# A graph network's last stage: all row gathers before all row scatters on one queue, and an earlier sum over the heads

## The chip, the cores and the metric

One core of one Trainium2 chip runs the kernel. Times are device microseconds of that core; the profile is of one execution, with times in microseconds from the start of its span. Engines: PE (matmuls and transposes), the vector engine (DVE), ACT (activations), POOL (here it only issues indirect DMAs), and SP (issues plain DMAs).

## The reference, cut to what matters

Two graph layers over 50,000 nodes of 96 features and 25,000 edges whose `dst` is sorted.

1. A message layer: rows of `x` at `src` and 32 edge features give messages and gates, their products are summed by `dst`, a small network updates each node, and two layer norms follow (the layer's own, then that of `x +` its output). The result is `x1`.
2. An attention layer, then a last norm:

```python
K, Q, V = x1 @ Wk + bk, x1 @ Wq + bq, x1 @ Wv + bv        # 8 heads of 12
E = edge_attr_96 @ We + be
score = exp(clip(sum_over_head(K[src] * Q[dst] / sqrt(12) * E), -5, 5))
h = segment_sum(V[src] * score, dst) / (segment_sum(score, dst) + 1e-6)
out = layernorm(x1 + h)
```

A node without an edge has h = 0; its output needs no attention and is written by the node update itself.

## The kernel before, in words

Edges go in 49 groups of 512, each as 4 tiles of 128 rows; nodes go in 49 groups of 1024. One SBUF array, `rows`, has a place for every tile of edges (196 tiles of 128 x 96).

The work has three compute stages (`edge_step`, `update_step`, `attend_step`, in each engine's block), and POOL's program is five passes over the 49 groups, four indirect DMAs of 128 rows for each group, written out without loops:

- line 375: rows of x at src into `rows` (edge stage);
- line 384: sums out of `rows` into `agg_d` at the last edge of each dst;
- line 398: rows of x1 at dst into `rows`. The two counts that say how many node groups must have been stored before it are read from SBUF into registers at the top of each group (`need_x1`);
- lines 410 and 420: the last stage, quoted below. It gathers rows of x1 at src for group g into `x1s` (four places in `x_in`, so it waits until PE has transposed group g - 4), and, eight groups behind, scatters the finished rows `fin` (four more places in `x_in`) of group g - 8 to `out`. Before the first scatter it waits until the node update has stored all of its own output.

```python
LAG = 8
for g in range(EGROUPS + LAG):
    if g < EGROUPS:
        if g >= XSLOTS:
            pool.wait_ge(ops_turned, 3 * (g - XSLOTS + 1))
        ...
    b = g - LAG
    ...
    if b >= 0:
        pool.wait_ge(fin_made, b + 1)
```

The attention stage itself takes one group a step. SP loads `x1d` (a copy of the group's part of `rows`, line 339), `ea` (edge features, line 344) and a mask (line 349, after the scan two groups back). PE, in `attend_step(i)`: K, Q, E and V products of group i (lines 557 to 566; V waits for the scan of group i - 1), the transposes back of the group before (line 572), twelve transposes of group i + 1 (helper `turn`, line 431: four of x1s, four of x1d, four of ea), and then the sum over the heads of `kqe` (line 586). ACT adds the bias to K (689), makes the final rows of group i - 3 (696), copies the three sets of transposes from PSUM (706), and takes exp (711). The vector engine makes `kq` (959), `kqe` (973), the division by the sums (988), the clip of the summed heads (998), the residual (1004), the norm's statistics (1009), the weighing of V (1016) and the running segment sum, a scan (1026), which carries over from group to group. Small operations of the norm are laid between them.

The update stage uses six double arrays of 128 x 768, `hg`, `xb`, `y`, `agg_in`, `x1o` and `oo`; nothing reads or writes them in the attention stage.

Of the kernel before, what the change touches and what calls it, by code (L numbers as in the profile page):

```python
# [25 lines left out]
P = 128  # L26
# [4 lines left out]
EJ = 4  # L31
# [13 lines left out]
XSLOTS = 4  # L45
FAR = 1 << 20
# [26 lines left out]
def per_slot(i, slot):  # L73

    return i * 8 + (16 - 8 * slot)
# [7 lines left out]
def build(nc, x, src, dst, ea32, ea96, mW1, mb1, mW2, mb2, gW1, gb1, gW2, gb2, uW1, ub1, uW2, ub2,  # L83
          ln_g, ln_b, Wq, bq, Wk, bk, We, be, Wv, bv, ident_c, heads_c, spare_c, bounds_c, out):
    with ExitStack() as ctx:
        def sb(name, shape, dt=F32):
            return ctx.enter_context(nc.sbuf_tensor(name, shape, dt))
# [37 lines left out]
        agg_in = sb("agg_in", [P, 2, NJ * D])  # L125
# [6 lines left out]
        hg, xb, y = (sb(n, [P, 2, NJ * D]) for n in ("hg", "xb", "y"))  # L132
        x1o, oo = sb("x1o", [P, 2, NJ * D]), sb("oo", [P, 2, NJ * D])
# [17 lines left out]
        x1s, fin = (x_in[:, :, k * EJ * D:(k + 1) * EJ * D].rearrange("p s (j f) -> p s j f", j=EJ) for k in range(2))  # L151
# [74 lines left out]
        lnb_placed = sem("lnb_placed")  # L226
        out_scattered = [[sem(f"out_scattered{t}_{j}") for j in range(EJ)] for t in range(2)]
# [21 lines left out]
        def _(sp):  # L249
# [83 lines left out]
            def attend_step(i, s, inner):  # L333
                if inner or i + 1 < EGROUPS:
                    if inner or i >= 1:
                        sp.wait_ge(ops_turned, i * 3)
                    for j in range(EJ):
                        sp.wait_ge(xd_gathered[1 - s][j], per_slot(i + 1, 1 - s))
                    sp.dma_start(x1d[:, 1 - s, :, :], rows[:, bass.DynSlice(i * EJ + EJ, EJ), :]).then_inc(x1d_loaded[1 - s], 16)
                    if isinstance(i, int) and i + 1 == EFULL:  # L340
                        sp.dma_start(ea[:, 1 - s, 0:ETAIL_J, :], ea96[EFULL * EROWS:TFULL * P, :].rearrange("(j p) f -> p j f", p=P)).then_inc(ea_loaded[1 - s], 16)
                        sp.dma_start(ea[0:ETAIL_P, 1 - s, ETAIL_J, :], ea96[TFULL * P:E, :]).then_inc(ea_loaded[1 - s], 16)
                    else:
                        sp.dma_start(ea[:, 1 - s, :, :], ea96[bass.DynSlice(i * EROWS + EROWS, EROWS), :].rearrange("(j p) f -> p j f", p=P)).then_inc(ea_loaded[1 - s], 16)
                if inner or i + 1 < EGROUPS:
                    sp.wait_ge(cont_stored, 48)
                    if inner or i >= 1:
                        sp.wait_ge(cscanned, i)
                    sp.dma_start(mask[:, 1 - s, :], cont_d[:, bass.DynSlice(i * EROWS + EROWS, EROWS)].broadcast_to([DH, EROWS])).then_inc(cmask_loaded[1 - s], 16)

            sweep(sp, -1, EGROUPS - 1, 3, 1, attend_step)
# [7 lines left out]
        def _(pool):  # L359
# [26 lines left out]

            pool.wait_ge(needs_made, 1)
            for g in range(EGROUPS):

                needs = [pool.value_load(need_x1[0:1, s, g:g + 1], min_val=16, max_val=slot_total(0)) for s in range(2)]  # L390
                for j in range(EJ):
                    pool.wait_ge(agg_added[g % 2][j], per_slot(g, g % 2))
                    if g >= 2:
                        pool.wait_ge(xd_gathered[g % 2][j], per_slot(g - 2, g % 2))
                for s in range(2):
                    pool.wait_ge(x1_stored[s], needs[s])
                for j in range(EJ):
                    pool.indirect_dma_start(rows[:, g * EJ + j, :], None, x1_d, rows_at(dst_at, g, j)).then_inc(xd_gathered[g % 2][j], 16)  # L398
            for s in range(2):
                pool.wait_ge(x1_stored[s], slot_total(s))  # L400

            LAG = 8
            for g in range(EGROUPS + LAG):
                if g < EGROUPS:
                    if g >= XSLOTS:
                        pool.wait_ge(ops_turned, 3 * (g - XSLOTS + 1))
                    for j in range(EJ):
                        if g >= 2:
                            pool.wait_ge(x1s_gathered[g % 2][j], per_slot(g - 2, g % 2))
                        pool.indirect_dma_start(x1s[:, g % XSLOTS, j, :], None, x1_d, rows_at(src_i, g, j)).then_inc(x1s_gathered[g % 2][j], 16)  # L410
                b = g - LAG
                if b == 0:
                    for s in range(2):
                        pool.wait_ge(out_stored[s], slot_total(s))
                if b >= 0:
                    pool.wait_ge(fin_made, b + 1)
                    for j in range(EJ):
                        if b >= 2:
                            pool.wait_ge(out_scattered[b % 2][j], per_slot(b - 2, b % 2))
                        pool.indirect_dma_start(out, rows_at(put_at, b, j), fin[:, b % XSLOTS, j, :], None,  # L420
                                                bounds_check=N - 1, oob_is_err=False).then_inc(out_scattered[b % 2][j], 16)
# [7 lines left out]
        def _(pe):  # L429
# [119 lines left out]

            def attend_step(i, q, inner):  # L550
# [23 lines left out]
                if inner or i + 1 < EGROUPS:  # L574
                    for j in range(EJ):
                        pe.wait_ge(x1s_gathered[1 - s][j], per_slot(i + 1, 1 - s))
# [15 lines left out]
        def _(act):  # L592
# [90 lines left out]
            def attend_step(i, q, inner):  # L683
# [6 lines left out]
                if inner or i >= 3:  # L690
                    act.wait_ge(cnorm_ready, i - 2)
                    if inner or i >= 7:
                        for j in range(EJ):
# [374 lines left out]
```

## Time and profile before

| what | value |
|---|---|
| runs of the kernel | 1256.85 us median of 3 (1254.91 to 1256.98) |
| the profiled execution | 1256.61 us, span 1254.8 us |
| busy: PE / DVE / ACT / POOL | 1030.6 / 956.2 / 688.5 / 946.5 us |
| granted PE clock, mean | 0.911 of full speed |
| packets of POOL's queue / SP's queue | 31,360 with 44.13 MB / 131,213 with 149.31 MB |
| POOL's last stage | from 750.49 us to the end |

The page gives busy time, not limits: an engine that is busy 80% may wait for another, and one that is busy 75% may have no pause that anything could fill. A group line tells the busy time and mean duration of like instructions, then the idle time of their engine just before them with what ended it; "issue" is idle time for which the profile shows no wait. A timeline line has start, duration, engine, line, operation, what is written and read, how many were merged, and in brackets the idle time before it.

### The profile page before, as it was taken

To read this page: it belongs to the slowest core of one execution; us is meant where nothing else is said; L and a number is where in the kernel's file an instruction comes from. 1 tells how busy PE (TensorE), PEld (TensorE's weight loads), DVE (VectorE), ACT (ScalarE), POOL (GpSimd) and SP (SyncE) were. 2 spreads that over 40 slices of the span, in tenths; PEclk is the share of its full clock that TensorE was granted. 3 is DMA by queue.
4 is the path that set the end of the run, shared out by engine and by line. 5 is a ranking of instruction groups with operands and counts; after the bars stand their busy time and mean duration, and the time that the engine had idled before them with its cause. 6 is when DMAs were issued, how large, how long until landed. Compare 5 with 4: busy or idle time off the path is not lost. (4 is left out here: it accounts for less than half of the span.)

```text
span 1254.8 us, 25004 instructions
## 1 busy us (share of the span) xinstructions
PE 1030.6 (82%) x5213; PEld 670.0 (53%) x5213; DVE 956.2 (76%) x4292; ACT 688.5 (55%) x1522; POOL 946.5 (75%) x984
## 2 busy tenths in 40 slices
PE   5999999989999999999999307788778877887770
PEld 2555555548877777777777303444444444443330
DVE  3544444437999999999999944888888788888883
ACT  2554545522687877778787743444444444444441
POOL 6777777777777777777777777777777777777777
PEclk9999999989999999999999758888888888888885
DMA  6787887544566666766677453334334333333320
GB/s 173 229 230 223 229 233 216 127 133 119 155 219 199 214 214 198 226 213 225 210 226 226 141 167 88 95 95 110 93 92 107 98 93 97 103 96 93 96 74 29
DMA packets 165371, 194.57 MB, mean 155 GB/s; under 512 B 102463, under 2 KB 111024, under 8 KB 165314
## 3 DMA queue, kind: packets, MB, share of 16 engines
q1 hardware_dynamic: 131213, 149.31, 38.4%
q0 software_dynamic: 31360, 44.13, 14.4%
q10 hardware_dynamic: 2740, 0.60, 0.3%
q14 instruction: 50, 0.40, 0.1%
q8 instruction: 8, 0.13, 0.0%
HBM read 101.21 MB, written 77.56 MB: 142 GB/s over the span
## 5 line engine op out<-in xcount | busy, mean ns | idle before, releaser
L384 POOL DMA_INDIRECT agg_d<-rows,put_at x196 | 193.5, 987 | 59.8 <-issue 47.3
L420 POOL DMA_INDIRECT out<-x_in,put_at x196 | 192.9, 984 | 59.7 <-issue 55.1
L410 POOL DMA_INDIRECT x_in<-agg_d,src_i x196 | 188.2, 960 | 62.0 <-issue 56.4
L398 POOL DMA_INDIRECT rows<-agg_d,dst_at x196 | 186.1, 950 | 62.4 <-issue 54.5
L375 POOL DMA_INDIRECT rows<-in_x,src_i x196 | 185.6, 947 | 62.4 <-issue 59.1
L658 ACT ACTIVATE x1o<-y,nshift,nscale 128x96 f32<-128x96 f32 x392 | 145.6, 454 | 87.5 <-DVE nshift L913 87.3
L696 ACT ACTIVATE x_in<-yc,cshift,cscale 128x96 f32<-128x96 f32 x196 | 75.5, 456 | 163.3 <-DVE cshift L1033 123.2
L431 PE MATMUL ps<-ident,x_in 128*96 128x128 f32 x588 | 93.8, 302 | 55.3 <-DMA x_in<-agg_d,src_i 54.1
L790 DVE SCALAR_TENSOR_TENSOR ps<-hidden,ps 96x512 f32<-96x512 f32 x49 | 33.9, 691 | 124.8 <-ACT hidden L637 124.8
L566 PE MATMUL ps<-nT,Wvs 96*104 96x512 f32 x98 | 59.3, 689 | 78.3 <-DVE seg L1026 78.2
L522 PE MATMUL ps<-uW2s,nT 97*128 97x96 f32 x784 | 98.6, 279 | 21.0 <-ACT nT L678 21.0
L870 DVE BATCH_NORM_STATS2 bn<-ps 128x6 f32<-128x96 f32 x392 | 100.3, 261 | 16.4 <-PE ps L522 16.1
L664 ACT ACTIVATE oo<-x1o,nscale 128x96 f32<-128x96 f32 x392 | 112.7, 361 | 0.0
L522 PEld LDWEIGHTS ps<-uW2s,nT 97*128 97x128 f32 x784 | 91.2, 191 | 31.8 <-ACT nT L678 31.8
L533 PEld LDWEIGHTS ps<-ident,agg_in 128*96 128x96 f32 x784 | 91.3, 163 | 26.7 <-issue 26.7
L431 PEld LDWEIGHTS ps<-ident,x_in 128*96 128x96 f32 x588 | 74.2, 142 | 56.8 <-issue 56.2
L888 DVE SCALAR_TENSOR_TENSOR y<-hg,nscale,xb 128x96 f32<-128x96 f32 x392 | 102.2, 311 | 0.6 <-issue 0.3
L530 PE MATMUL ps<-einT,uW1x 96*96 96x512 f32 x196 | 97.2, 619 | 1.2 <-ACT einT L650 1.2
L539 PE MATMUL ps<-centre,einT 96*128 96x96 f32 x784 | 94.2, 273 | 0.0
L533 PE MATMUL ps<-ident,agg_in 128*96 128x128 f32 x784 | 93.9, 273 | 0.0
L924 DVE BATCH_NORM_STATS2 bn<-y 128x6 f32<-128x96 f32 x392 | 93.7, 252 | 0.2 <-issue 0.2
L539 PEld LDWEIGHTS ps<-centre,einT 96*128 96x128 f32 x784 | 91.4, 192 | 0.0
(147 smaller groups left out, 2248.1 us busy)
## 6 DMA issues: line engine op xcount, KB each, us to landing
agg_d<-zeros SPq DMA_DIRECT2D x40, 480.0 KB
x_in<-in_x SPq DMA_DIRECT2D x49, 384.0 KB
agg_in<-agg_d SPq DMA_DIRECT2D x49, 384.0 KB
agg_d<-x1o SPq DMA_DIRECT2D x49, 384.0 KB
out<-oo SPq DMA_DIRECT2D x49, 384.0 KB
mask<-cont_d SPq DMA_DIRECT2D x49, 208.0 KB
ein<-rows SPq DMA_DIRECT2D x49, 192.0 KB
mask<-cont_d SPq DMA_DIRECT2D x49, 192.0 KB
```

Source lines behind the costliest of these rows:

```text
L375: pool.indirect_dma_start(rows[:, g * EJ + j, :], None, x, rows_at(src_i, g, j)).then_inc(xs_gathered[g % 2][j], 16)
L384: pool.indirect_dma_start(agg_d, rows_at(put_at, g, j), rows[:, g * EJ + j, :], None, bounds_check=N - 1, oob_is_err=False).then_inc(agg_a ...
L398: pool.indirect_dma_start(rows[:, g * EJ + j, :], None, x1_d, rows_at(dst_at, g, j)).then_inc(xd_gathered[g % 2][j], 16)
L410: pool.indirect_dma_start(x1s[:, g % XSLOTS, j, :], None, x1_d, rows_at(src_i, g, j)).then_inc(x1s_gathered[g % 2][j], 16)
L420: pool.indirect_dma_start(out, rows_at(put_at, b, j), fin[:, b % XSLOTS, j, :], None, bounds_check=N - 1, oob_is_err=False).then_inc(out_s ...
L431: mmx = pe.transpose(to, of, ident[:, :])
L522: m = pe.matmul(ps[:, 4 + 2 * s + j // 4, (j % 4) * D:(j % 4 + 1) * D], nT[:, s, j * P:(j + 1) * P], uW2s[:, :], start=False, stop=j % 4 == 3)
L533: m = pe.matmul(ps[0:D, 2 + j // 4, (j % 4) * P:(j % 4 + 1) * P], agg_in[:, 1 - s, j * D:(j + 1) * D], ident[:, :], start=False, stop=j % ...
L539: m = pe.matmul(ps[:, 4 + 2 * (1 - s) + j // 4, (j % 4) * D:(j % 4 + 1) * D], xT[:, j // 4, (j % 4) * P:(j % 4 + 1) * P], centre[:, :], st ...
L658: o = act.activation(x1o[:, s, j * D:(j + 1) * D], y[:, s, j * D:(j + 1) * D], ACT.Identity, bias=nshift[:, k, j:j + 1], scale=nscale[:, k ...
L664: o = act.activation(oo[:, 1 - s, j * D:(j + 1) * D], x1o[:, 1 - s, j * D:(j + 1) * D], ACT.Identity, scale=nscale[:, k, 2, j:j + 1])
L888: b = dve.scalar_tensor_tensor(y[:, s, at], hg[:, s, at], nscale[:, 1 - s, 0, j:j + 1], xb[:, s, at], ALU.mult, ALU.add)
```

## The change

POOL's last stage becomes two passes. The gathers of x1 at src run for all groups first, into 24 places named `ahead` that lie over the six update arrays (now one array `node_work`, in the order hg, xb, y, agg_in, x1o, oo); the first 16 places need hg, xb, y and agg_in to be free, and the wait for the update's own output moves to group 16. From group 24 on a gather waits until group g - 24 has been copied away. SP copies each group from its place in `ahead` to the four places of `x1s` by a plain DMA (new semaphores `x1s_loaded`), between its copies for x1d and ea, and PE waits for that copy instead of the gather. All scatters follow in a second pass. ACT writes its final rows into `rows`, in the place of their group, and the scatters read them there; ACT's wait for earlier scatters is gone.

On PE, the sum over the heads of group i comes after the first four of the twelve transposes of group i + 1, not after all twelve. In the pass at dst, POOL reads the next group's two counts behind the first two gathers of a group. SP's attention loop is written out.

```diff
-        agg_in = sb("agg_in", [P, 2, NJ * D])
...
-        hg, xb, y = (sb(n, [P, 2, NJ * D]) for n in ("hg", "xb", "y"))
-        x1o, oo = sb("x1o", [P, 2, NJ * D]), sb("oo", [P, 2, NJ * D])
+        node_work = sb("node_work", [P, 6, 2, NJ * D])
+        hg, xb, y, agg_in, x1o, oo = (node_work[:, k, :, :] for k in range(6))
...
-            def attend_step(i, s, inner):
...
+            for g in range(EGROUPS):
+                s = g % 2
+                if g >= 2:
+                    sp.wait_ge(ops_turned, (g - 1) * 3)
+                for j in range(EJ):
+                    sp.wait_ge(xd_gathered[s][j], per_slot(g, s))
+                sp.dma_start(x1d[:, s, :, :], rows[:, g * EJ:(g + 1) * EJ, :]).then_inc(x1d_loaded[s], 16)
+                for j in range(EJ):
+                    sp.wait_ge(x1s_gathered[s][j], per_slot(g, s))
+                sp.dma_start(x1s[:, g % XSLOTS, :, :], ahead[:, g % AHEAD, :, :]).then_inc(x1s_loaded[g % XSLOTS], 16)
...
             pool.wait_ge(needs_made, 1)
+            needs = [need_of(0, s) for s in range(2)]
             for g in range(EGROUPS):
-
-                needs = [pool.value_load(need_x1[0:1, s, g:g + 1], min_val=16, max_val=slot_total(0)) for s in range(2)]
...
                 for j in range(EJ):
                     pool.indirect_dma_start(rows[:, g * EJ + j, :], None, x1_d, rows_at(dst_at, g, j)).then_inc(xd_gathered[g % 2][j], 16)
+                    if j < 2 and g + 1 < EGROUPS:
+                        needs.append(need_of(g + 1, j))
...
-            LAG = 8
-            for g in range(EGROUPS + LAG):
...
+            for g in range(EGROUPS):
+                if g == AHEAD_FREE:
                     for s in range(2):
                         pool.wait_ge(out_stored[s], slot_total(s))
-                if b >= 0:
...
+                if g >= AHEAD:
+                    pool.wait_ge(x1s_loaded[(g - AHEAD) % XSLOTS], per_slot4(g - AHEAD, (g - AHEAD) % XSLOTS))
+                for j in range(EJ):
+                    if g >= 2:
+                        pool.wait_ge(x1s_gathered[g % 2][j], per_slot(g - 2, g % 2))
+                    pool.indirect_dma_start(ahead[:, g % AHEAD, j, :], None, x1_d, rows_at(src_i, g, j)).then_inc(x1s_gathered[g % 2][j], 16)
+
+            for g in range(EGROUPS):
+                pool.wait_ge(fin_made, g + 1)
+                for j in range(EJ):
+                    if g >= 2:
+                        pool.wait_ge(out_scattered[g % 2][j], per_slot(g - 2, g % 2))
+                    pool.indirect_dma_start(out, rows_at(put_at, g, j), rows[:, g * EJ + j, :], None,
+                                            bounds_check=N - 1, oob_is_err=False).then_inc(out_scattered[g % 2][j], 16)
...
                     for b, (of, t) in enumerate(((x1s, (q + 1) % XSLOTS), (x1d, 1 - s), (ea, 1 - s))):
+                        if b == 1:
+                            sum_heads(i, inner)
                         for j in range(EJ):
                             turn(ps[0:D, b, j * P:(j + 1) * P], of[:, t, j, :], ops_turned if j == EJ - 1 else None)
-                if inner or 0 <= i < EGROUPS:
-                    pe.wait_ge(kqe_made, i + 1)
-                    pe.matmul(ps[0:DH, 5, :], heads[:, :], kqe[:, :], start=True, stop=True).then_inc(heads_summed, 1)
+                else:
+                    sum_heads(i, inner)
...
-                    if inner or i >= 7:
-                        for j in range(EJ):
-                            act.wait_ge(out_scattered[1 - s][j], per_slot(i - 7, 1 - s))
                     for j in range(EJ):
-                        o = act.activation(fin[:, (q + 1) % XSLOTS, j, :], yc[:, 1 - s, j, :], ACT.Identity,
+                        o = act.activation(rows[:, bass.DynSlice(i * EJ - 3 * EJ + j, 1), :].rearrange("p a f -> p (a f)"), yc[:, 1 - s, j, :], ACT.Identity,
```

## Rows read from the trace of the kernel before

**Rows 1.** Page, first lines: span, busy time of each engine and its share.
```profile
span 1254.8 us, 25004 instructions
...
PE 1030.6 (82%) x5213; PEld 670.0 (53%) x5213; DVE 956.2 (76%) x4292; ACT 688.5 (55%) x1522; POOL 946.5 (75%) x984
```

**Rows 2.** Page, groups by line, POOL's passes; busy, mean ns, idle before.
```profile
L384 POOL DMA_INDIRECT agg_d<-rows,put_at x196 | 193.5, 987 | 59.8 <-issue 47.3
L420 POOL DMA_INDIRECT out<-x_in,put_at x196 | 192.9, 984 | 59.7 <-issue 55.1
L410 POOL DMA_INDIRECT x_in<-agg_d,src_i x196 | 188.2, 960 | 62.0 <-issue 56.4
L398 POOL DMA_INDIRECT rows<-agg_d,dst_at x196 | 186.1, 950 | 62.4 <-issue 54.5
```

**Rows 3.** Timeline of POOL, start of the last stage: start us, us, what, idle before.
```profile
750.49 0.94 POOL L410 DMA_INDIRECT x_in<-agg_d,src_i  x1 [0.30 <-issue]
...
789.26 0.94 POOL L410 DMA_INDIRECT x_in<-agg_d,src_i  x1 [0.30 <-issue]
792.75 0.94 POOL L410 DMA_INDIRECT x_in<-agg_d,src_i  x1 [2.54 <-PE ps L431]
```

**Rows 4.** Timeline of POOL, gathers and scatters in turn.
```profile
1156.12 1.01 POOL L420 DMA_INDIRECT out<-x_in,put_at  x1 [0.30 <-issue]
1157.43 0.99 POOL L420 DMA_INDIRECT out<-x_in,put_at  x1 [0.30 <-issue]
1158.73 0.97 POOL L420 DMA_INDIRECT out<-x_in,put_at  x1 [0.30 <-issue]
...
1161.28 0.99 POOL L410 DMA_INDIRECT x_in<-agg_d,src_i  x1 [0.30 <-issue]
...
1166.35 1.01 POOL L420 DMA_INDIRECT out<-x_in,put_at  x1 [0.30 <-issue]
```

**Rows 5.** Timeline of POOL, the last scatters.
```profile
1211.18 0.97 POOL L420 DMA_INDIRECT out<-x_in,put_at  x1 [0.30 <-DMA out<-x_in,put_at]
...
1252.06 0.97 POOL L420 DMA_INDIRECT out<-x_in,put_at  x1 [0.30 <-issue]
```

**Rows 6.** Timeline of the vector engine, four of the 49 scans.
```profile
771.13 1.22 DVE L1026 TENSOR_TENSOR_SCAN seg<-mask,ps 104x512 f32<-104x512 f32 x1
...
796.41 1.28 DVE L1026 TENSOR_TENSOR_SCAN seg<-mask,seg,ps 104x512 f32<-104x512 f32 x1
...
806.08 1.28 DVE L1026 TENSOR_TENSOR_SCAN seg<-mask,seg,ps 104x512 f32<-104x512 f32 x1
...
1226.39 1.28 DVE L1026 TENSOR_TENSOR_SCAN seg<-mask,seg,ps 104x512 f32<-104x512 f32 x1
```

**Rows 7.** Timeline of PE: x1d transposes and heads of a step.
```profile
799.92 1.06 PE L431 MATMUL ps<-ident,x1d 128*96 128x128 f32 x4
...
801.63 1.43 PE L586 MATMUL ps<-hidden,heads 96*104 96x512 f32 x2
```

**Rows 8.** Timeline of the vector engine, same step: kqe, clip, weighing.
```profile
798.77 0.74 DVE L973 SCALAR_TENSOR_TENSOR hidden<-ps,bes,hidden 96x512 f32<-96x512 f32 x1
...
803.09 0.69 DVE L998 TENSOR_SCALAR hidden<-ps 104x512 f32<-104x512 f32 x1 [1.96 <-PE ps L586]
...
805.29 0.75 DVE L1016 SCALAR_TENSOR_TENSOR ps<-ps,bvs,score 104x512 f32<-104x512 f32 x1
```

**Rows 9.** Timeline of ACT: last copy and exp of that step; last results.
```profile
801.87 0.59 ACT L706 ACTIVATE einT<-ps 96x512 f32<-96x512 f32 x1 [0.26 <-PE ps L431]
803.82 0.63 ACT L711 ACTIVATE score<-hidden 104x512 f32<-104x512 f32 x1 [1.35 <-DVE hidden L998]
...
1236.66 1.54 ACT L696 ACTIVATE x_in<-yc,cshift,cscale 128x96 f32<-128x96 f32 x4 [2.14 <-DVE cshift L1033]
```

**Rows 10.** Timeline of SP's queue: the x1d load after a scan.
```profile
798.76 0.50 SPq L339 DMA_DIRECT2D x1d<-rows  x1
```

**Rows 11.** Page, DMA issues: KB each, median us from issue to landing.
```profile
ea<-in_edge_attr SPq DMA_DIRECT2D x48, 192.0 KB, 3.3
```

More of the change, by code:

```diff
@@ L45 @@
 XSLOTS = 4
+AHEAD = 24
+AHEAD_FREE = 16
 FAR = 1 << 20
@@ L148, in build @@
         seg = sb("seg", [DH, 2, EROWS])
-        x1s, fin = (x_in[:, :, k * EJ * D:(k + 1) * EJ * D].rearrange("p s (j f) -> p s j f", j=EJ) for k in range(2))
+        x1s = x_in[:, :, 0:EJ * D].rearrange("p s (j f) -> p s j f", j=EJ)
+        ahead = node_work[:, :, :, :].rearrange("p k s f -> p (k s f)").rearrange("p (r j f) -> p r j f", j=EJ, f=D)
         x1d = sb("x1d", [P, 2, EJ, D])
@@ L226, in build @@
         lnb_placed = sem("lnb_placed")
+        x1s_loaded = [sem(f"x1s_loaded{s}") for s in range(XSLOTS)]
         out_scattered = [[sem(f"out_scattered{t}_{j}") for j in range(EJ)] for t in range(2)]
@@ L330, in _ @@
             sweep(sp, -3, NGROUPS + 6, 9, 10, update_step, XSLOTS)
-            def attend_step(i, s, inner):
-                if inner or i + 1 < EGROUPS:
-                    if inner or i >= 1:
-                        sp.wait_ge(ops_turned, i * 3)
-                    for j in range(EJ):
[L338 to L349, printed above, removed]
@@ L351, in _ @@
-            sweep(sp, -1, EGROUPS - 1, 3, 1, attend_step)
+            for g in range(EGROUPS):
[8 more added lines that the diff above has]
+                sp.dma_start(x1s[:, g % XSLOTS, :, :], ahead[:, g % AHEAD, :, :]).then_inc(x1s_loaded[g % XSLOTS], 16)
+                if g == EFULL:
+                    sp.dma_start(ea[:, s, 0:ETAIL_J, :], ea96[EFULL * EROWS:TFULL * P, :].rearrange("(j p) f -> p j f", p=P)).then_inc(ea_loaded[s], 16)
+                    sp.dma_start(ea[0:ETAIL_P, s, ETAIL_J, :], ea96[TFULL * P:E, :]).then_inc(ea_loaded[s], 16)
+                else:
+                    sp.dma_start(ea[:, s, :, :], ea96[g * EROWS:(g + 1) * EROWS, :].rearrange("(j p) f -> p j f", p=P)).then_inc(ea_loaded[s], 16)
+                sp.wait_ge(cont_stored, 48)
+                if g >= 2:
+                    sp.wait_ge(cscanned, g - 1)
+                sp.dma_start(mask[:, s, :], cont_d[:, g * EROWS:(g + 1) * EROWS].broadcast_to([DH, EROWS])).then_inc(cmask_loaded[s], 16)
@@ L385, in _, with need_of @@
                                             bounds_check=N - 1, oob_is_err=False).then_inc(agg_added[g % 2][j], 16)
+            def need_of(g, s):
+                return pool.value_load(need_x1[0:1, s, g:g + 1], min_val=16, max_val=slot_total(0))
             pool.wait_ge(needs_made, 1)
+            needs = [need_of(0, s) for s in range(2)]
             for g in range(EGROUPS):
[L390 removed]
                 for j in range(EJ):
@@ L396, in _ @@
                     pool.wait_ge(x1_stored[s], needs[s])
+                needs = []
                 for j in range(EJ):
                     pool.indirect_dma_start(rows[:, g * EJ + j, :], None, x1_d, rows_at(dst_at, g, j)).then_inc(xd_gathered[g % 2][j], 16)
+                    if j < 2 and g + 1 < EGROUPS:
+                        needs.append(need_of(g + 1, j))
             for s in range(2):
                 pool.wait_ge(x1_stored[s], slot_total(s))
-            LAG = 8
-            for g in range(EGROUPS + LAG):
[L404 to L412, printed above, removed]
+            for g in range(EGROUPS):
+                if g == AHEAD_FREE:
@@ L413, in _ @@
                     for s in range(2):
                         pool.wait_ge(out_stored[s], slot_total(s))
-                if b >= 0:
[L416 to L421, printed above, removed]
+                if g >= AHEAD:
+                    pool.wait_ge(x1s_loaded[(g - AHEAD) % XSLOTS], per_slot4(g - AHEAD, (g - AHEAD) % XSLOTS))
@@ L548, in _, with sum_heads @@
             pe.wait_ge(hg_made, NGROUPS)
+            def sum_heads(i, inner):
+                if inner or 0 <= i < EGROUPS:
+                    pe.wait_ge(kqe_made, i + 1)
+                    pe.matmul(ps[0:DH, 5, :], heads[:, :], kqe[:, :], start=True, stop=True).then_inc(heads_summed, 1)
             def attend_step(i, q, inner):
@@ L574, in attend_step @@
                 if inner or i + 1 < EGROUPS:
-                    for j in range(EJ):
-                        pe.wait_ge(x1s_gathered[1 - s][j], per_slot(i + 1, 1 - s))
+                    pe.wait_ge(x1s_loaded[(q + 1) % XSLOTS], per_slot4(i + 1, (q + 1) % XSLOTS))
                     pe.wait_ge(x1d_loaded[1 - s], per_slot(i + 1, 1 - s))
@@ L581, in attend_step @@
                     for b, (of, t) in enumerate(((x1s, (q + 1) % XSLOTS), (x1d, 1 - s), (ea, 1 - s))):
+                        if b == 1:
+                            sum_heads(i, inner)
                         for j in range(EJ):
                             turn(ps[0:D, b, j * P:(j + 1) * P], of[:, t, j, :], ops_turned if j == EJ - 1 else None)
-                if inner or 0 <= i < EGROUPS:
-                    pe.wait_ge(kqe_made, i + 1)
-                    pe.matmul(ps[0:DH, 5, :], heads[:, :], kqe[:, :], start=True, stop=True).then_inc(heads_summed, 1)
+                else:
+                    sum_heads(i, inner)
             sweep(pe, -1, EGROUPS + 1, 4, 2, attend_step, XSLOTS)
```

2 lines of the change are left out of this document (1 added, 1 removed).

## The prediction, on record before the changed kernel ran

> **What bounds the kernel now.** I read the page first: of a span of 1254.8 us the engine with matmuls is busy 82%, the vector engine 76%, POOL 75% [rows 1]. That ranks the engines wrongly, because POOL has no real idle time. Grouped by line, its passes of 196 indirect DMAs (four of the five are shown) have 186 to 194 us busy and 60 to 62 us idle in front of them, nearly all put down to "issue" [rows 2]. The POOL timeline tells what that idle time is: one indirect DMA of 0.94 to 1.01 us, then 0.30 us, then the next, whatever the other engines do [rows 3, 4]. So 980 indirect DMAs at about 1.28 us each make 1254 us: the kernel is as long as POOL's list of them, and a change is worth what it takes out of that list. The last scatter starts at 1252.06 and takes 0.97 [rows 5], so it ends at 1253.03; 1.77 us of span follow it (its data landing and the last waits), and the profiled execution's 1256.61 us has 1.81 us outside the span. The median of the runs, 1256.85, lies 0.24 above the profiled one; I make the sum against 1256.61.
>
> **POOL in the last stage.** It runs from 750.49 to 1253.03, with three patterns.
>
> - Gathers alone: from 750.49 to 789.26 lie 31 starts, 38.77 us, so one gather every 1.2506 us [rows 3].
> - Scatters alone: from 1211.18 to 1252.06 lie 32 starts, 40.88 us, so one every 1.2775 us [rows 5]. Only the attention step's last three groups run beside most of them; the 0.97 of the third scatter in the mixed part, where everything else runs, is the same [rows 4].
> - Four of the one and four of the other in turn: from 1156.12 to 1166.35, 10.23 us for eight [rows 4]. Four gathers and four scatters at their own pitches would take 4 x 1.2506 + 4 x 1.2775 = 10.11 us. The missing 0.12 us sits in the two instructions behind each change of kind: scatters 1.01 and 0.99 against 0.97, the first gather 0.99 against 0.94 [rows 3, 4], the second a little less.
>
> And one stall: at 792.75 POOL had waited 2.54 us for the transposes of group 4, because the gather of group 8 reuses its place; 0.30 of it is the usual gap, so 2.24 is lost [rows 3].
>
> **The change on POOL.** All 196 gathers now run first, so 245.1 us (196 x 1.2506); then one change of kind, 0.05 (the 0.04 and 0.02 of [rows 4]); then 196 scatters, of which the last starts 195 x 1.2775 = 249.1 us on and takes 0.97. From 750.49 that ends at 1245.7, against 1253.03: **7.3 us less**. Item by item it is the same: 41 rounds of eight lose 0.12 each, 4.9 us, and the stall 2.24. The group rows bear it out: the last stage's gathers have a mean of 960 ns and not 0.94, its scatters 984 and not 970 [rows 2]. The agg_d scatters of line 384, which are not mixed with gathers, still show 987 [rows 2]; they run beside the update's large transfers, so I keep that as a bound: 196 x 0.017 = 3.3 us of the gain would be missing if the new scatters ran so.
>
> **What must be ready in time.** Gathers of groups 24 and up wait for the copy of group g-24 out of its place. The gather of group 48 starts at 750.49 + 192 x 1.2506 = 990.6. SP issues the copy of group 24 behind the 22nd scan, as it issues its loads two steps ahead today; at 9.5 us a step and with the start worked out below that is 775.6 + 9.5 x 21 = 975, landed by 979. That holds, with 12 us to spare. The out_stored wait, now at group 16, falls at 831, long after the last store, as before. Scatter of group b starts at 995.7 + 5.11 b and needs group b's result; the last one starts at 1240.9.
>
> The attention part sets its own pace. Its 49 scans run from 771.13 to 1226.39, 9.48 us apart on average [rows 6]; the last results are done at 1236.66 + 1.54 = 1238.2, 11.8 us behind the last scan [rows 9]. Two of the edits touch it.
>
> First, the rows of src now come by an extra 192 KB copy on SP's queue, 49 of them. The first transposes start today as soon as the gather of group 0 lands. Now an issue of 0.5 for the copy comes in between, one of 0.5 for ea, which is behind it in the queue, and a landing of 3.3 us as ea's [rows 10, 11]; with what lies between them I take 4.5: the first step starts that much later, the first scan at 775.6. Later copies cost nothing: SP issues the loads of a group right after a scan (798.76, behind the scan of 796.41 that the interval to 806.08 starts with [rows 6, 10]), three issues of some 0.7 with the gaps and 3.3 land them by about 804, and the transposes that need them start some four microseconds behind that (the step before has its at 799.92, one step of 9 to 10 us earlier [rows 7]). What waits behind a late copy on SP is ea and the mask of the same group; that slack covers them too.
>
> Second, the sum over the heads moves ahead of eight transposes. In the step that ends with the scan at 806.08, the x1d transposes start at 799.92 and the heads at 801.63; the clip starts 1.46 behind, at 803.09, after the vector engine was idle for 1.96 us [rows 7, 8]. Moved, the heads start at 799.92 and the clip at 801.4 (799.92 + 1.46). The remaining transposes, and ACT's last copy, today at 801.87 + 0.59, move back by the heads' time, up to 1.43; exp, which is behind the copies on ACT, then starts at 803.9 at the latest, as it does today at 803.82 [rows 9]. The weighing today starts 1.47 behind it at 805.29 because other work of the vector engine lies between [rows 8]; that work is now done earlier, so it can start once exp is done, at 804.5. The step gets some 0.8 us shorter, 9.67 to 8.9. By that the last result comes at 775.6 + 48 x 8.9 + 11.8 = 1214.6, 26 us before POOL wants it. PE's new wait for kqe costs nothing while kqe is made by then; what queues behind it are the eight transposes, and ACT waits for those.
>
> ACT writes its results into rows rather than x_in: same shape, same 1.54 us for four. It also loses its wait for earlier scatters; ACT isn't on the path, so I count nothing.
>
> The two register reads per group in the xd pass move behind its first two gathers. That pass has 62.4 us of idle time against 59.8 for the agg_d pass [rows 2], 2.6 us more in a few gaps. If the reads cause them, up to 2.6 is gained; if they now hold up a gather instead of hiding under one, as much is lost. I take 0, since nearly all gaps of that pass are the same 0.30.
>
> **Sum.** 1256.61 - 7.3 = 1249.3; with the median's 0.24 kept partly, **1249.4 us**, 0.6% less. A measurement of this kernel can tell about 0.2% (2.5 us) from no change.
>
> **A page that speaks against it.** What the trace shows first: in the mixed part a scatter takes 0.97 at the third place of its four, the same as in the last scatters with the vector engine nearly done [rows 4, 5]. The Trainium skill, "SBUF — State Buffer", section "SBUF: two separate sides", says that GpSimd cannot write descriptors while the vector engine runs an instruction that takes both shared ports. By that rule the long instructions would be collisions with the vector engine, and ordering the passes would not remove them. That is rival two.
>
> **Rivals.**
>
> 1. *The attention part ends last, slower.* Place: PE's wait for kqe in front of eight transposes. If kqe came about 1.7 us after the first four transposes, the heads would be no earlier than now, and everything behind them would be later by their time, about 1.2 us a step: 9.48 + 1.2 = 10.7. Last result at 775.6 + 48 x 10.7 + 11.8 = 1301, then four scatters, 5 us: some 1309 us. It decides from a step of 9.45 us up (1240.9 - 11.8 - 775.6 = 453.5 over 48), and the kernel is slower than before by what can be told from 9.65. Against it: in the step shown kqe is ready at 798.77 + 0.74 = 799.5, before the first four transposes are through at 799.92, and the vector engine is idle 1.96 us before the clip [rows 7, 8]. 5%.
> 2. *The change doesn't remove the long instructions*, because collisions and not changes of kind cause them. Only the stall goes: 1254.4 us. Against it: they stand right behind a change of kind in the two changes shown, and are absent from the ends of the run of scatters [rows 4, 5]. 7%.
> 3. *The step keeps its 9.48.* The last result comes at 775.6 + 455.3 + 11.8 = 1242.7, 1.8 after POOL wants it: 1251.2 us. For it: the 0.8 us was read from one step; where PE's four transposes take less than the 1.06 shown there, less stands behind the heads. 8%.
> 4. *The gaps in the xd pass go as well*: 2.6 more, 1246.8 us. 12%.
>
> The forecast itself gets 66%; 2% is for what I don't see. The range takes in the forecast, rivals 3 and 4 and the bound of 3.3 us on the scatters (1252.7): 1246.3 to 1252.7. Faster by over 0.2%: forecast, 3, 4 and a share of the rest, 88%; within it: rival 2, 7%; slower: rival 1, 5%.
>
> **What would show it.** In the new profile: POOL's gather group at a mean near 944 ns and its scatters near 971 ns; idle before either near 59 us each, with no wait for PE; no wait of POOL for ACT's results or for x1s_loaded over 0.3 us; the first scatter of out near 995.7 and the last near 1244.7; scans 8.3 to 9 us apart, the last before 1215; the clip's idle wait for PE gone or shorter. If POOL shows a wait for line 696's results, rival 1 or 3 holds; if the means stay at 960 and 984, rival 2; if the xd pass's idle time falls to 60, rival 4. The forecast is wrong if the time is over 1252.7 or under 1246.3.

## The result, and the profile after

The changed kernel takes 1248.29 us (median of 6 runs, 1246.98 to 1249.54) against 1255.81 us for the one before in the same comparison: ratio 0.9944, 95% interval 0.9934 to 0.9954. Forecast were 1249.4 us and a range of 1246.3 to 1252.7. The profiled execution took 1249.49 us, 7.1 less than the profiled one of before. Three executions on record (one of the kernel before, one each of heads_last and reads_none below) took over 110 us longer than their fellows; all medians and ratios here leave them out.

The page of the changed kernel: span, busy times, and POOL's groups (busy us, mean ns, idle before). Line 387 was 384, 426 was 420, 404 was 398 and 419 was 410 [rows 1, 2].

```profile
span 1247.7 us, 24758 instructions
...
PE 991.4 (79%) x5213; PEld 629.4 (50%) x5213; DVE 951.6 (76%) x4292; ACT 688.6 (55%) x1522; POOL 941.2 (75%) x984
...
L387 POOL DMA_INDIRECT agg_d<-rows,put_at x196 | 193.4, 987 | 59.7 <-issue 46.3
L426 POOL DMA_INDIRECT out<-rows,put_at x196 | 190.7, 973 | 59.7 <-issue 36.0
L404 POOL DMA_INDIRECT rows<-agg_d,dst_at x196 | 186.2, 950 | 63.1 <-issue 56.7
...
L419 POOL DMA_INDIRECT node_work<-agg_d,src_i x196 | 185.1, 944 | 59.7 <-issue 54.5
```

Gathers fell from 960 to 944 ns each and scatters from 984 to 973; their idle time is 59.7 us for both passes, so the stall is gone. The agg_d pass (387) is as it was; the pass at dst (404) has 0.7 us more idle time.

POOL's timeline, where the gathers end and the scatters begin, and at the end [compare rows 4, 5]:

```profile
994.59 0.94 POOL L419 DMA_INDIRECT node_work<-agg_d,src_i  x1 [0.30 <-issue]
995.84 1.01 POOL L426 DMA_INDIRECT out<-rows,put_at  x1 [0.30 <-issue]
997.15 0.99 POOL L426 DMA_INDIRECT out<-rows,put_at  x1 [0.30 <-issue]
998.45 0.97 POOL L426 DMA_INDIRECT out<-rows,put_at  x1 [0.31 <-issue]
```

```profile
1244.97 0.97 POOL L426 DMA_INDIRECT out<-rows,put_at  x1 [0.30 <-issue]
```

There is one change of kind left, with its 1.01 and 0.99. The first scatter starts at 995.84 (forecast 995.7), the last ends at 1245.94 (forecast 1245.7), though the stage begins 0.55 us later than the forecast had it. It takes 494.9 us from 751.04, where it took 502.5. Of these 7.65 us, 5.37 are busy time (3.11 of the gathers, 2.26 of the scatters) and 2.29 idle time of the gathers, the stall.

The attention part: first and last scan (DVE), last results (ACT) [rows 6, 9], and PE and DVE in one step [rows 7, 8].

```profile
776.98 1.22 DVE L1034 TENSOR_TENSOR_SCAN seg<-mask,ps 104x512 f32<-104x512 f32 x1
...
1169.73 1.28 DVE L1034 TENSOR_TENSOR_SCAN seg<-mask,seg,ps 104x512 f32<-104x512 f32 x1
```

```profile
1180.09 1.54 ACT L704 ACTIVATE rows<-yc,cshift,cscale 128x96 f32<-128x96 f32 x4 [2.21 <-DVE cshift L1041]
```

```profile
907.25 1.10 PE L577 MATMUL ps<-nT,Wvs 96*104 96x512 f32 x2 [0.48 <-DVE seg L1034]
...
908.56 0.60 PE L437 MATMUL ps<-ident,x_in 128*96 128x128 f32 x4
909.54 1.10 PE L559 MATMUL ps<-hidden,heads 96*104 96x512 f32 x2 [0.39 <-DVE hidden L981]
910.49 0.60 PE L437 MATMUL ps<-ident,x1d 128*96 128x128 f32 x4
```

```profile
908.75 0.74 DVE L981 SCALAR_TENSOR_TENSOR hidden<-ps,bes,hidden 96x512 f32<-96x512 f32 x1
...
911.27 0.68 DVE L1006 TENSOR_SCALAR hidden<-ps 104x512 f32<-104x512 f32 x1
```

The scans are 8.18 us apart, (1169.73 - 776.98) / 48, where they were 9.48, and the last results are there at 1181.6, 59 us before POOL asks for the last group. The clip (line 1006) has no idle time in front of it, here and in all steps but the first. The vector engine is busy for 7.9 us of a step of 8.2, so it now sets the step; it was busy for the same 7.9 of 9.6 before. The price of the order is in the same rows: the heads wait 0.39 us for kqe, which is made at 908.75 + 0.74.

### The profile page after: what moved, and what is told of

It is laid out like the page before. It is cut to its first block and busy times, and to the rows that moved or that the text cites. A ratio compares the mean times of both kernels' runs of the same rounds, so it can differ in the third digit from the quotient of the medians.

```text
span 1247.7 us, 24758 instructions
## 1 busy us (share of the span) xinstructions
PE 991.4 (79%) x5213; PEld 629.4 (50%) x5213; DVE 951.6 (76%) x4292; ACT 688.6 (55%) x1522; POOL 941.2 (75%) x984
## 5 line engine op out<-in xcount | busy, mean ns | idle before, releaser
L387 POOL DMA_INDIRECT agg_d<-rows,put_at x196 | 193.4, 987 | 59.7 <-issue 46.3
L426 POOL DMA_INDIRECT out<-rows,put_at x196 | 190.7, 973 | 59.7 <-issue 36.0
L419 POOL DMA_INDIRECT node_work<-agg_d,src_i x196 | 185.1, 944 | 59.7 <-issue 54.5
L669 ACT ACTIVATE node_work<-node_work,nshift,nscale 128x96 f32<-128x96 f32 x392 | 145.7, 454 | 86.9 <-DVE nshift L921 86.8
L704 ACT ACTIVATE rows<-yc,cshift,cscale 128x96 f32 (+1 forms) x196 | 75.5, 456 | 98.8 <-DVE cshift L1041 98.8
L675 ACT ACTIVATE node_work<-node_work,nscale 128x96 f32<-128x96 f32 x392 | 112.7, 361 | 0.0
L539 PEld LDWEIGHTS ps<-ident,node_work 128*96 128x96 f32 x784 | 92.7, 165 | 27.3 <-issue 27.3
L896 DVE SCALAR_TENSOR_TENSOR node_work<-node_work,nscale 128x96 f32<-128x96 f32 x392 | 102.5, 312 | 0.7 <-issue 0.3
L539 PE MATMUL ps<-ident,node_work 128*96 128x128 f32 x784 | 95.2, 275 | 0.0
L932 DVE BATCH_NORM_STATS2 bn<-node_work 128x6 f32<-128x96 f32 x392 | 93.8, 252 | 0.2 <-issue 0.2
L714 ACT ACTIVATE nT<-ps 96x512 f32<-96x512 f32 x99 | 56.0, 589 | 66.9 <-PE ps L437 55.0
```

The costliest lines, as they stand in the source:

```text
L387: pool.indirect_dma_start(agg_d, rows_at(put_at, g, j), rows[:, g * EJ + j, :], None, bounds_check=N - 1, oob_is_err=False).then_inc(agg_a ...
L419: pool.indirect_dma_start(ahead[:, g % AHEAD, j, :], None, x1_d, rows_at(src_i, g, j)).then_inc(x1s_gathered[g % 2][j], 16)
L426: pool.indirect_dma_start(out, rows_at(put_at, g, j), rows[:, g * EJ + j, :], None, bounds_check=N - 1, oob_is_err=False).then_inc(out_sca ...
L539: m = pe.matmul(ps[0:D, 2 + j // 4, (j % 4) * P:(j % 4 + 1) * P], agg_in[:, 1 - s, j * D:(j + 1) * D], ident[:, :], start=False, stop=j % ...
L669: o = act.activation(x1o[:, s, j * D:(j + 1) * D], y[:, s, j * D:(j + 1) * D], ACT.Identity, bias=nshift[:, k, j:j + 1], scale=nscale[:, k ...
L675: o = act.activation(oo[:, 1 - s, j * D:(j + 1) * D], x1o[:, 1 - s, j * D:(j + 1) * D], ACT.Identity, scale=nscale[:, k, 2, j:j + 1])
```

## The experiments

| kernel | median us | ratio to before (95%) |
|---|---|---|
| changed, with the prediction | 1248.29 | 0.9944 (0.9934 to 0.9954) |
| lag8_four | 1254.12 | 0.9989 (0.9980 to 0.9998) |
| lag8_one | 1262.42 | 1.0058 (1.0046 to 1.0070) |
| heads_last | 1250.11 | 0.9963 (0.9949 to 0.9976) |
| ahead16 | 1274.21 | 1.0149 (1.0134 to 1.0164) |
| after_again (changed) | 1249.56 | 0.9954 (0.9940 to 0.9968) |
| reads_top | 1248.85 | 0.9945 (0.9931 to 0.9960) |
| reads_none | 1255.92 | 1.0006 (0.9997 to 1.0016) |
| y_one_input | 1244.97 | 0.9919 (0.9904 to 0.9933) |
| after_third (changed) | 1249.41 | 0.9956 (0.9943 to 0.9970) |
| heads_last_again | 1251.03 | 0.9966 (0.9953 to 0.9979) |
| heads_only | 1253.75 | 0.9994 (0.9983 to 1.0005) |
| reads_exact | 1247.29 | 0.9941 (0.9927 to 0.9954) |

The rows from lag8_four to ahead16 share their runs of the kernel before; so do the next four, and the last four. The changed kernel itself stands in the second and third group (after_again, after_third); lag8_four to ahead16 are compared with it through the kernel before. y_one_input leaves work out, and reads_none and reads_exact are right for this input only.

### Does the order of kinds carry the gain?

The last stage's issue order alone, on top of the changed kernel:

```diff
-            for g in range(EGROUPS):
-                if g == AHEAD_FREE:
...
-            for g in range(EGROUPS):
-                pool.wait_ge(fin_made, g + 1)
...
+            LAG = 8
+            for g in range(EGROUPS + LAG):
+                for j in range(EJ):
+                    if g < EGROUPS:
+                        gather(g, j)
+                for j in range(EJ):
+                    if g >= LAG:
+                        scatter(g - LAG, j)
```

> The changed kernel with only POOL's order of the last stage put back: four gathers of group g, then four scatters of group g-8, over the same 24 places and with the same copies. Theory A (a change of kind makes the two instructions behind it longer): each round of eight takes 10.23 us and not 10.11, 41 rounds lose 4.9 us, so 1248.3 + 4.9 = 1253.2 us, gather mean near 960 ns and scatter mean near 984 ns, no stall at the start of the stage. Rival B (collisions with the vector engine): the long instructions do not depend on the order, means 944 and 973 as in the changed kernel, 1248.3 us. Rival C (the gain came from the places alone, that is from the 2.24 us stall and what follows it): 1248.3 us too, with the means of A not seen.

Measured: 1254.12 us. POOL's two groups of that kernel (page):

```profile
L428 POOL DMA_INDIRECT out<-rows,put_at x196 | 193.1, 985 | 59.7 <-issue 55.5
...
L418 POOL DMA_INDIRECT node_work<-agg_d,src_i x196 | 188.3, 961 | 59.8 <-issue 59.2
```

The means are back at 961 and 985 with the places, copies and the early heads all kept, and there is no stall. Theory A had 960 and 984; B and C fall. The last stage takes 500.6 us in this profile, 5.7 more than in the changed kernel's. All 81 changes of kind in it look alike: behind the change a scatter takes 1.009 us, the second 0.992, the third and fourth 0.974; gathers take 0.995, 0.968 and then 0.947 (means). The median is 0.9 above the forecast of 1253.2. What makes the 0.9 is open: the profiled execution, at 1257.12 us the longest of the eleven, can't tell.

In the second kernel the two inner loops are one:

```diff
-                for j in range(EJ):
-                    if g >= LAG:
+                    if g >= LAG:
                         scatter(g - LAG, j)
```

> As lag8_four, but one gather and one scatter in turn, so that every instruction of the mixed part stands right behind a change of kind. Theory A: gathers 0.99 us and scatters 1.01 us throughout the mixed part (some 164 of each), 0.05 x 164 + 0.04 x 164 = 14.8 us more than the changed kernel: 1263 us, or 10 us more than lag8_four. Rival B: durations as in the changed kernel, 1248.3 us.

Measured: 1262.42 us. From POOL's timeline of that kernel:

```profile
1101.23 0.97 POOL L418 DMA_INDIRECT node_work<-agg_d,src_i  x1 [0.30 <-issue]
1102.51 1.01 POOL L428 DMA_INDIRECT out<-rows,put_at  x1 [0.30 <-issue]
1103.82 0.98 POOL L418 DMA_INDIRECT node_work<-agg_d,src_i  x1 [0.30 <-issue]
```

Every instruction of the mixed part is long now. Scatters take the full 1.01, but a gather behind a single scatter takes 0.97 to 0.98 and not the 0.99 it takes behind four: POOL's busy time in the stage rose by 11.3 us (190.3 + 196.8 against 185.1 + 190.7) and not by 14.8. The rest of the 14.1 us that the stage got longer is a wait of 3.06 us (2.76 of it loss) for ACT's first results before the first scatter, which this order asks for earlier. So the time came out right, partly by luck: one term was too large and one was left out.

### Are the 24 places needed?

```diff
-AHEAD = 24
+AHEAD = 16
```

> The changed kernel with 16 places and not 24. Theory (a gather waits for the copy out of its place, two steps ahead of PE): the copy of group 32 is issued near 786.4 + 28 x 8.18 = 1015.5 and lands some 3.5 us later, and the gather of group 48 cannot start before 1019, where it starts at 990 now; the scatters follow, 28 us later: about 1277 us. Rival (copies run far enough ahead, the number of places does not bind): 1248.3 us.

Measured: 1274.21 us. From POOL's timeline:

```profile
961.80 0.94 POOL L419 DMA_INDIRECT node_work<-agg_d,src_i  x1 [3.80 <-DMA x_in<-node_work]
963.04 0.94 POOL L419 DMA_INDIRECT node_work<-agg_d,src_i  x1 [0.30 <-issue]
...
970.25 0.94 POOL L419 DMA_INDIRECT node_work<-agg_d,src_i  x1 [3.77 <-DMA x_in<-node_work]
```

Once a group, from group 40 on, POOL waits for the copy (x_in<-node_work) of the group 16 before, 29.7 us in 9 waits (27.0 of it loss): the gathers go at the attention part's 8.2 us a group and not at 5. The first gather of group 48 starts at 1018.96 (forecast: not before 1019), the gathers end near 1023.7 and the scatters follow. This profiled execution took 1277.43 us, as forecast; the median is 2.8 us below it. With 24 places no gather waits: in the changed kernel's profile the copy of group 24 is issued at 949.72 and group 48's gather starts at 990.84, so the forecast's margin of 12 us was in fact over 35.

### What is the place of the heads worth?

```diff
                     for b, (of, t) in enumerate(...):
-                        if b == 1:
-                            sum_heads(i, inner)
                         ...
-                else:
-                    sum_heads(i, inner)
+                sum_heads(i, inner)
```

> The changed kernel with the sum over the heads behind all twelve transposes again. Theory (the step goes back to about 9.48 us and the attention part ends last): first scan 777.0, last scan near 777.0 + 48 x 9.48 = 1232, last results 11.9 us later at 1244 where POOL wants them at 1241.1: 3 us more, about 1251.3 us, and a wait of POOL for line 704 in the last groups. Rival (step length is set by something else and stays near 8.2 us, or the order of the heads does not matter at all): 1248.3 us, last results near 1182.

Measured: 1250.11 us. In its profile the step is 9.40 us, the last scan at 1225.32 and the last results at 1237.2, 4.6 us before POOL takes the last group, and POOL never waits:

```profile
1241.78 0.97 POOL L426 DMA_INDIRECT out<-rows,put_at  x1 [0.30 <-issue]
```

So here the forecast wait did not come: the first scan was at 773.91 and not at 777, and the step was 9.40 us and not 9.48. The same kernel once more:

> The same kernel as heads_last, once more beside the changed kernel on one chip. Theory (its attention part, at 9.40 us a step, ends 4.6 us before POOL wants the last result, so the place of the heads is worth nothing in the time): the same as the changed kernel within 1 us, and no wait of POOL for line 701. Rival (in some executions it ends late and the time is a few us more): 2 to 3 us above the changed kernel.

Measured: 1251.03 us, 1.6 above the changed kernel beside it (after_third), the intervals overlapping. In this profile the first scan is at 776.42, the step 9.44 us, and POOL waits, near the end, for ACT's results of one group:

```profile
1233.61 0.97 POOL L426 DMA_INDIRECT out<-rows,put_at  x1 [2.70 <-ACT rows L701]
```

2.40 of the 2.70 is loss. The theory had no such wait, so it falls, and the rival holds in kind. Both profiles together say where this kernel stands: on the edge, with a margin from 4.6 us down to less than nothing from one execution to the next. The early heads are worth some 1 to 2 us here, as insurance; the two medians of the kernel, 1.6 and (against the changed kernel's first runs, not beside it) 1.8 us above the changed one, fit that and by themselves don't prove it. What they change in a step is told at the end.

The same edit on the kernel before, alone:

> The kernel before with the sum over the heads moved and nothing else. Theory (the first steps get shorter, 6.9, 7.4 and 7.6 us as in the changed kernel, so group 4 is transposed by 790.4 when POOL wants its place at 790.5; the order of gathers and scatters still costs its 4.9 us): the stall of 2.24 us goes or falls below 0.5, 1253 us. Rival (the last eight transposes now come behind the heads, so the place becomes free no earlier): stall and time as before, 1255.2 us.

Measured: 1253.75 us, ratio 0.9994 with 1 in its interval. The stall went down, but not away:

```profile
792.86 0.94 POOL L410 DMA_INDIRECT x_in<-agg_d,src_i  x1 [1.56 <-PE ps L431]
```

1.26 us is lost in place of 2.24, and the theory had under 0.5. That would be one microsecond of gain, as the medians have it (1253.75 against 1254.69), though the interval does not exclude none. The first 16 steps are short (6.9 to 8.5 us), until they have caught up with the gathers; from then on they take 10.2 us, POOL's pace for eight instructions. Alone the edit has nothing to shorten.

### The register reads

The reads went back to the top of the group (reads_top), and then away, with waits on constants (reads_none):

```diff
-            needs = [need_of(0, s) for s in range(2)]
             for g in range(EGROUPS):
+                needs = [need_of(g, s) for s in range(2)]
...
-                    if j < 2 and g + 1 < EGROUPS:
-                        needs.append(need_of(g + 1, j))
```

```diff
-                needs = [need_of(g, s) for s in range(2)]
+                needs = [min(16 * ((g + 4) // 2), slot_total(s)) for s in range(2)]
```

> The changed kernel once more, unchanged, beside the others of this call on the same chip, as the level that they are compared with: 1248.3 us by both theories.

> The changed kernel with the two register reads of the pass at dst back at the top of each group, as before the change. In the profile before that pass had 62.4 us of idle time, after 63.1, each with some gaps over 0.36 us. Theory (the place of the reads decides nothing): idle time of that pass between 61.9 and 64.7 as in the five profiles so far, time within 1 us of the changed kernel. Rival (the moved reads hold up the gathers behind them): the gaps at the second and third gather of a group go, 1 us less.

> The changed kernel with the register reads left out: the pass at dst waits on constants instead, for two to three node groups more than a group of edges needs with this input (so it is right for this input only). Theory (the extra idle time of that pass comes from the register reads): all gaps over 0.36 us go, idle time 59.7 as in the other passes, 3 to 4 us less, near 1244.8 us. Rival (the gaps come from something else that happens at those times, such as the code of other engines or the transfers of the node update): idle time stays at 62 to 65, 1248.3 us.

Measured: 1249.56, 1248.85 and 1255.92 us. No effect of the place of the reads shows: the times agree within 0.8 us, and the idle time of that pass is 61.7 and 62.6 us. Reads_none was slower, since its constants were too strict: near the end of the pass POOL waited 3.5 us twice for the node update's stores (agg_d<-node_work). The group of its page:

```profile
L403 POOL DMA_INDIRECT rows<-agg_d,dst_at x196 | 186.6, 952 | 67.0 <-issue 51.5
```

The small gaps before that were gone in it, except one of 1.11 us, which looked like my theory. So the exact constants, from a table EXACT written out for this input:

```diff
-                needs = [min(16 * ((g + 4) // 2), slot_total(s)) for s in range(2)]
+                needs = (16 * EXACT[g][0], 16 * EXACT[g][1])
```

> The changed kernel, unchanged, as the level for this call: 1248 to 1250 us.

> As reads_none, with the constants that the registers would hold for this input (right for this input only), so that no wait is stricter than in the changed kernel. Theory (the register reads make the gaps): idle time of the pass at dst 60 to 60.8 us, at most the gap of group 36 left, 1.5 to 2.5 us less than the changed kernel. Rival (reads_none lacked the gaps because its stricter waits moved POOL): gaps as in the changed kernel, same time.

Measured: 1249.41 and 1247.29 us. The page of reads_exact:

```profile
L404 POOL DMA_INDIRECT rows<-agg_d,dst_at x196 | 186.0, 949 | 62.6 <-issue 55.1
```

The idle time is 62.6 us, with gaps of 1.50, 0.73, 0.69 and 1.12 us. My theory falls: the gaps come without register reads too. The median is 2.1 us below the changed kernel's, but the intervals of the ratios overlap, and it is right for one input only. What makes the gaps (0.4 to 2.7 us each, 2 to 5 us a pass, never in the agg_d pass under the same update) stays open; that they fall near the same times in most profiles (645, 660, 685) is all that I can say.

### Why are the agg_d scatters 987 ns?

My range held 3.3 us for the case that the new scatters would take what line 384's took, "beside the update's large transfers". In the changed kernel's profile the long ones stand beside something else as well, the vector engine's y operation, the only large one with two inputs in SBUF (hg and xb). POOL, then DVE:

```profile
347.50 0.97 POOL L387 DMA_INDIRECT agg_d<-rows,put_at  x1 [0.30 <-issue]
348.78 1.14 POOL L387 DMA_INDIRECT agg_d<-rows,put_at  x1 [0.30 <-issue]
```

```profile
348.19 0.78 DVE L896 SCALAR_TENSOR_TENSOR node_work<-node_work,nscale 128x96 f32<-128x96 f32 x3
```

Of the 147 such scatters that start between 310 and 500 us, 93 meet no y operation and have a mean of 0.972. Of the 54 that do, only those are longer that start while a y operation is already running with more than 0.13 us to go: 30, of which 29 take 0.99 to 1.14. The other 24 (y begins after the scatter, or is nearly through) take 0.97 to 0.98. The rows show one of each: the scatter at 347.50 was under way when y began, the one at 348.78 was not. Most of the 29 are longer by what was left of y at their start, less 0.13 us.

```diff
-... nscale[:, 1 - s, 0, j:j + 1], xb[:, s, at], ALU.mult, ALU.add)
+... nscale[:, 1 - s, 0, j:j + 1], ps[:, 4 + 2 * s, EJ * D:(EJ + 1) * D], ALU.mult, ALU.add)
```

> The changed kernel with the second SBUF input of the vector engine's y operation (line 896) replaced by a row in PSUM; it leaves the residual x out of the first norm, everything else is done as before. In the profiles the scatters to agg_d take 0.97 us where no such operation runs beside them and up to 1.14 where one does. Theory (an operation with two SBUF inputs holds POOL up): the scatters to agg_d take 0.97 to 0.98 throughout, mean 973 and not 987, that pass 2.5 to 3 us shorter, a little more in the pass at dst: 1245 us. Rival (the transfers of the node update do it): mean stays at 987, 1248.3 us.

Measured: 1244.97 us, 4.6 less than the changed kernel beside it (0.9919, interval 0.9904 to 0.9933, against 0.9954, 0.9940 to 0.9968). Its page:

```profile
L387 POOL DMA_INDIRECT agg_d<-rows,put_at x196 | 190.5, 972 | 59.7 <-issue 46.6
L404 POOL DMA_INDIRECT rows<-agg_d,dst_at x196 | 185.1, 944 | 63.1 <-issue 55.3
```

The agg_d scatters are at 972 and the gathers at dst went from 951 to 944. Between 310 and 500 us again 54 scatters meet a y operation, and now all take 0.97 to 0.98. The transfers are the same, so the theory is confirmed and the rival is out. The Trainium skill, "SBUF — State Buffer", section "Who interferes with whom", states that a vector-engine instruction with two SBUF inputs contends with a GpSimd instruction that reads SBUF; by these rows the trace agrees, at 0.02 to 0.17 us a collision. I have no version that does this without leaving work out: xb would have to lie in PSUM, whose eight banks that stage's code all uses. It wasn't tried.

## Why the prediction was right, point by point

- *POOL's list of indirect DMAs is the time.* Right. In every kernel here the time follows POOL's list: means up, time up; a wait of POOL, time up. An edit on PE or the vector engine shows in the time only through POOL: by a wait (heads_last_again) or by the length of its instructions (y_one_input).
- *7.3 us less: 41 x 0.12 and a stall of 2.24.* Right. The stage got shorter by 7.65 us, 5.37 by shorter instructions and 2.29 by the stall (forecast 4.9 and 2.24); lag8_four took back 5.7 of it by the profiles (by its ratio against the three of the changed kernel, 4.1 to 5.6 us) with the order alone, and its stall stayed away.
- *Rival two, collisions with the vector engine.* Wrong for this stage, since the long instructions follow the order (lag8_four, lag8_one). Collisions exist in another one, with the y operation. What I had put down to transfers, the 987 of line 384, was that. The bound of 3.3 us in my range was there for a wrong reason: the attention stage has no large operation of that kind, only small ones of the norm (128 x 4).
- *Places and the copy.* Right: 24 hold, 16 cost some 26 us. The first transposes came at 762.02, 5.0 later and not 4.5; the first scan came at 776.98 (forecast 775.6), and between 773.5 and 778.2 in the other kernels with the copy, reads_none apart.
- *The attention step, 8.9 us and last results at 1214.6.* Mis-sized: 8.18 us and 1181.6. I had costed the step with PE's durations of one slow step (1.06 for four transposes, [rows 7]) and took these as given. They were the clock's: that step ran at a granted clock of 0.82, and the change brought the attention part's steps to 1.00, which the forecast did not have (last section). It lay under POOL either way, so the time could not show the error.
- *Rival three, the step keeps its 9.48, 1251.2 us.* It did not happen, but it holds as a statement on what happens without the early heads: heads_last and its repeat gave 1250.11 and 1251.03, with a loss of 2.40 us in one profile of two. So the forecast had some luck: the step got shorter by a mechanism that was not in it, and without that the time would have been about where this rival put it.
- *Rival four, and the 0 for the register reads.* 0 fits (reads_top). The 2.6 us in the pass at dst were a real excess, but reads_exact has 62.6 us too, without the reads.
- *Rival one* did not show: PE waited 0.39 us for kqe in the step above, 0.46 in the worst, not 1.7.

## What to carry to other kernels

Where an engine issues without a pause, subtract its pitch from every pattern it runs in: what a mixed order costs over the pure ones can be read from one timeline, before anything is built. Moving work so that such a queue runs one kind at a time needs places for what comes early, and their number follows from the consumer's pace (places = lead of the queue over the consumer at its worst point). An edit off that queue is worth its slack: measure it in the kernel that needs the slack, not alone. And a duration on PE that is read from one step holds for that step's granted clock: look at the clock before you carry it over.

## What the runs showed that was not expected

- Behind a change between gather and scatter, POOL's next two instructions are longer: scatters 1.01 and 0.99 us against 0.97, gathers 0.99 and 0.97 against 0.94; with single ones in turn 1.01 and 0.97 to 0.98. All 81 changes of lag8_four's profile show it. Whether POOL itself does it, or the transfers of the other kind that are still under way, was not tried.
- A vector-engine instruction with two SBUF inputs (y) that was already running stretched indirect DMAs on POOL from 0.97 to as much as 1.14 us; one that began after them did not. Without it POOL's busy time over the two passes is 4.6 us less than in after_again, beside it, and 3.9 less than in the changed kernel's first profile.
- The order of PE's work moved its clock. In the first 245 us of the last stage the granted clock was 0.84 before and 0.96 after (busy time by engine in that stretch, before and then after; the last three numbers are granted clock, DMA share and GB/s):

```profile
750.00:995.00 245.00, 192.85 (x662) 105.31 (x663) 189.18 (x812) 109.35 (x217) 184.54 (x192) 0.84 0.36 96
```

```profile
750.00:995.00 245.00, 191.23 (x737) 91.57 (x738) 211.35 (x919) 121.73 (x244) 185.29 (x197) 0.96 0.51 136
```

With the heads last it was 0.85 again (0.84 in the repeat), with all else as in the changed kernel. Two neighbouring steps of heads_last, from scan to scan:

```profile
864.70:874.56 9.86, 7.88 (x26) 4.37 (x26) 7.99 (x35) 4.53 (x9) 7.57 (x8) 0.83 0.48 122
874.56:882.75 8.19, 6.37 (x26) 3.14 (x26) 7.77 (x36) 4.31 (x9) 6.06 (x8) 1.00 0.49 134
```

All steps of this kernel but the last fall into two kinds. Those at a granted clock of 1.00 (12) take 7.6 to 8.4 us; those with a stretch at the lower level, 0.82 or 0.83 of full speed on average (35), take 9.7 to 9.9. The kernel before has the same two kinds in its first 41 steps. The new order is at 1.00 in all steps but the last and takes 8.18 us on average. So once the steps have settled, a step of the old order at full clock takes about what the new one takes (8.0 to 8.4 us), and nearly all of the 1.3 us a step that the change saved goes with the clock. These are single steps between slower ones, though; no run holds the old order at full clock. By its place alone the early sum saves something in the first steps only, where both orders run at 1.00: 7.57 and 8.00 us with the heads last, 6.94 and 7.44 with them early. Four transposes take 0.60 us in 144 of 147 cases now, as at 2.4 GHz; before, 57 took that, and 76 took 1.06, as at 1.2.

- What else differs is PE's idle time. Before, and with the heads last, it comes in one piece of up to 2.1 us a step in front of the V product, where PE waits for the scan, 1.95 us on average. Now it is 1.6 us a step in several pieces of at most 0.8: 0.6 in front of V, 0.7 for ACT's copies, 0.2 for kqe (means of 30 steps). That this is what holds the clock up is only the likely reading; no run varied it alone. The early heads don't hold it up everywhere: in heads_only, once the steps go at POOL's pace, the clock is at 0.78 to 0.89 in nearly all of them, with single waits of PE of up to 3.8 us.
